# Down-projection LoRA and mix tables split once into DRAM during the gate/up pairs, and gathered ready-made two tiles ahead

## The reference

```
def lora_add(base, inp, A, B):
    t = einsum('bri,bni->bnr', A[idx], inp)
    return base + einsum('bor,bnr->bno', B[idx], t) * 0.5
gate = lora_add(x @ W_gate.T, x, A_gate, B_gate)        # 512 -> 1376
up   = lora_add(x @ W_up.T,   x, A_up,   B_up)
act  = silu(gate) * up
x = x + lora_add(act @ W_down.T, act, A_down, B_down)   # 1376 -> 512
x = x + einsum('bct,bcd->bdt', x, W[cond])              # 32 x 32 per sequence
```

## Time and profile before

| | us |
|---|---|
| median of 3 runs | 446.88 (446.78 to 447.9) |
| the profiled execution | 446.79 |
| its span in the trace | 445.0 |
| PE busy | 438.1 (98% of the span) |
| DVE busy | 335.2 (75%) |
| ACT busy | 212.3 (48%) |
| POOL busy | 169.7 (38%) |

### The profile page before, as it was taken

The page is one execution under the profiler, slowest core; times in us unless marked ns, Lnnn a source line. Parts: engine busy times, 40 slices in busy tenths (PEclk is TensorE's granted clock), DMA queues, the critical chain, the costliest instruction groups (busy, mean ns, idle before and its releaser), DMA issues.

```text
span 445.0 us, 7248 instructions
## 1 busy us (share of the span) xinstructions
PE 438.1 (98%) x2475; PEld 393.5 (88%) x2475; DVE 335.2 (75%) x623; ACT 212.3 (48%) x397; POOL 169.7 (38%) x156
## 2 busy tenths in 40 slices
PE   8989999999999999999999999999999999999997
PEld 6877888888888888888888888999999999999996
DVE  6779999878867867857857858978667767766665
ACT  6746355366444544543543444843454454444531
POOL 2722223121121221121121452675776666756620
PEclk9999999999999999999999999999999999999999
DMA  8975664356555665665565599947776665556631
GB/s 243 381 242 146 181 172 114 109 172 188 145 181 151 159 172 145 161 173 144 159 173 144 145 287 340 247 138 202 215 201 208 208 180 178 177 178 196 191 96 47
DMA packets 99843, 81.12 MB, mean 182 GB/s; under 512 B 50944, under 2 KB 83200, under 8 KB 99808
## 3 DMA queue, kind: packets, MB, share of 16 engines
q1 hardware_dynamic: 88512, 47.27, 37.9%
q0 software_dynamic: 11008, 33.30, 24.8%
q10 hardware_dynamic: 288, 0.10, 0.1%
HBM read 65.18 MB, written 15.47 MB: 181 GB/s over the span
## 4 chain that ended last, share of the span: by engine, by line
PE 92%; DMA 2%; POOL 2%; issue 2%; DVE 1%; ACT 1%; SPq 0%; POOLq 0%
PE bank L1384 28%; PE bank L1262 9%; PE bank L1263 9%; PE bank L1261 9%; PE bank L1216 7%; PE bank L1217 7%; PE bank L1218 7%; PE bank L1283 4%; PE bank L1284 4%; PE bank L1414 2%; POOL a_raw L453 2%; PE bank L1394 2%; DMA b_raw<-in_b_rows,rows 2%; DMA gu_landing<-in_w_gate 1%; PE bank L1399 1%
## 5 line engine op out<-in xcount | busy, mean ns | idle before, releaser
L453 POOL DMA_INDIRECT b_raw<-in_b_rows,rows x48 | 51.8, 1078 | 188.7 <-DVE b_gu L803 188.1
L1384 PE MATMUL bank<-wd,actT_hi 128*128 128x288 f32 (+1 forms) x636 | 109.9, 295 | 0.0
L1384 PEld LDWEIGHTS bank<-wd,actT_hi 128*128 128x128 f32 (+1 forms) x636 | 93.8, 188 | 1.4 <-issue 0.2
L453 POOL DMA_INDIRECT a_dn_raw<-in_a_dn_rows,rows x64 | 77.3, 1208 | 19.5 <-issue 19.5
L803 DVE SCALAR_TENSOR_TENSOR b_gu<-b_raw,low_rows,b_gu 128x1024 fp32r<-128x1024 f32 (+1 forms) x48 | 55.6, 1159 | 26.8 <-ACT b_gu L513 26.8
L1384 PE MATMUL bank<-wd,actT_lo 128*128 128x288 f32 (+1 forms) x318 | 68.1, 296 | 0.0
L513 ACT ACTIVATE b_gu<-b_raw 128x1024 fp32r<-128x1024 f32 (+1 forms) x48 | 46.2, 963 | 11.2 <-DMA b_raw<-in_b_rows,rows 9.8
L1384 PEld LDWEIGHTS bank<-wd,actT_lo 128*128 128x128 f32 (+1 forms) x318 | 51.0, 188 | 0.0
L603 ACT ACTIVATE act<-bank 128x512 f32<-128x512 f32 (+1 forms) x48 | 26.1, 546 | 41.4 <-PE bank L1284 41.4
L910 DVE TENSOR_TENSOR act<-act,bank 128x512 f32<-128x512 f32 (+1 forms) x48 | 29.8, 621 | 8.6 <-PE bank L1284 7.8
L799 DVE TENSOR_TENSOR actT_lo<-actT_raw,actT_hi 128x1280 fp32r<-128x1280 f32 (+1 forms) x32 | 27.0, 886 | 11.6 <-ACT actT_hi L513 11.6
(11 more groups left out here) (180 smaller groups left out, 1004.2 us busy)
## 6 DMA issues: line engine op xcount, KB each, us to landing
actT_raw<-actT_dram SPq DMA_DIRECT2D x16, 640.0 KB
actT_dram<-staging SPq DMA_DIRECT2D x64, 128.0 KB, 2.9
x_sb<-in_x SPq DMA_DIRECT2D x16, 256.0 KB, 2.9
xT_raw<-in_xT SPq DMA_DIRECT2D x15, 256.0 KB, 2.7
out<-out_sb SPq DMA_DIRECT2D x15, 256.0 KB
a_raw<-in_a_gu_rows SPq DMA_DIRECT2D x56, 64.0 KB, 2.7
actT_dram<-staging SPq DMA_DIRECT2D x32, 88.0 KB, 3.2
wd_raw<-in_w_down SPq DMA_DIRECT2D x10, 256.0 KB, 5.9
```

Of the source, the lines that this page charges most:

```text
L453: return pool.indirect_dma_start(dst, None, src, bass.IndirectOffsetOnAxis(ap=rows[:, tile, col:col + 1], axis=0))
L1384: last = pe.matmul(ps_down[e][half][:, 0:HALF], a[e][0:n, c, :], wd[0:n, c, part, at:at + HALF], start=(c == 0 and i == 0), stop=(c == NC ...
```

## The change

- **Tables.** Three internal DRAM tensors hold the high and the low part of all A_down rows (`a_table`, parts side by side in a row), all B_down rows (`b_table`, high rows and then low rows) and all mix matrices (`mix_table`). To the mix matrices the identity is added first, so the mix product gives `x + x W` in one.
- **Rounds.** The tables are made in seven rounds (`ROUNDS`): four of A_down (four adapters each, 128x704, 352 KB), two of B_down (128x512, 256 KB), one of the mix (128x128). A round is: SP loads it into `a_dn_raw[0]` (`load_round`), ACT writes the high part into `a_dn_raw[1]`, DVE writes the low part over `a_dn_raw[0]` (both `split_round`), SP stores both (`store_round`). All rounds use the same two buffers, so the load of a round waits until the stores of the one before it have landed (`tables_stored`).
- **Where they stand.** `rounds_of(pr)` gives pair 3 a late round 0, pair 4 an early round 1 and a late round 2, pair 5 rounds 3 and 4, pair 6 rounds 5 and 6. Early: on ACT after `split_b(pr, 1, 0)`, on DVE ahead of `gating(pr, 1)`. Late: on ACT ahead of `split_b(pr, 2, 0)`, on DVE after `add_u7`, ahead of `split_b(pr, 2, 0)`. SP stores the early round and loads the late one after `spill(pr, 0)`, and stores the late one and loads the next after `spill(pr, 1)`.
- **POOL.** The first gather of A_down, ahead of pair 7, waits until every round has been stored.
- **Down stage.** From tile 2 on the A_down rows come split from `a_table` into `a_pair` (two tiles ahead), and ACT only copies both parts; B_down comes split into `b_dn[e]`; the mix parts come by four DMAs of SP (`load_mix`, each with a register load). `split_b_dn`, `split_mix`, DVE's part of `split_a_dn` and `residual_out` are gone; ACT copies the output (`copy_out`). PE issues the same matmuls in the same order.

```diff
+            def load_round(i):
+                reached(sp, tables_stored, 32 * i)
+                if i < A_ROUNDS:
+                    sp.dma_start(a_dn_raw[0][:, :, :], a_round(i)).then_inc(table_landed, 16)
...
+            def store_round(i):
+                cols, tables = table_parts(i)
+                n = A_DN if i < A_ROUNDS else H if i < A_ROUNDS + 2 else CH
+                sp.wait_ge(table_ready, i + 1)
+                for part, to in enumerate(tables):
+                    src = table_sb(1 - part, cols, n if len(to.shape) == 3 else None)
+                    sp.dma_start(to, src).then_inc(tables_stored, 16)
...
+            def load_mix(m, e):
+                reached(sp, mix_done, 2 * (m - 1))
+                for q in range(TILE_SEQS):
...
                     spill(pr, s)
+                    if s == 0:
+                        if early is not None:
+                            store_round(early)
+                        if late is not None:
+                            load_round(late)
+                    else:
+                        if late is not None:
+                            store_round(late)
+                            if late + 1 < ROUNDS:
+                                load_round(late + 1)
...
             def gather_a_dn(m, q0=0, q1=TILE_SEQS):
-                reached(pool, a_dn_ready, m - 1)
+                if m == 0 and q0 == 0:
+                    pool.wait_ge(tables_stored, 32 * ROUNDS)
+                if m == 2:
+                    for t in range(2):
+                        pool.wait_ge(section_done[t], NS * PAIRS)
+                reached(pool, a_dn_copied, m - 3)
...
+            def split_round(i):
+
+                if i < ROUNDS - 1:
+                    sc.wait_ge(table_landed, 16 * (i + 1))
+                else:
+                    sc.wait_ge(table_mix_added, 1)
+                cols, _ = table_parts(i)
+                hi(table_sb(1, cols).bitcast(F32R), table_sb(0, cols)).then_inc(table_hi_ready, 1)
...
                     split_down(0, 3)
+                late = rounds_of(pr)[1]
+                if late is not None:
+                    split_round(late)
                 split_b(pr, 2, 0)
...
-            def split_mix(m, e):
...
+            def copy_out(m, e):
+                sc.wait_ge(mix_done, 2 * (m + 1))
+                reached(sc, stored[e], 16 * (m // 2))
+                hi(out_sb[e][:, :], ps_mix[:, 0:H]).then_inc(out_ready, 1)
```

More of the change, by code:

```diff
@@ L79, in build @@
         a_raw = [sb(f"a_raw{t}", [P, TILE_SEQS, A_GU]) for t in range(2)]
+        with ExitStack() as then:
+            a_pair = [sb(f"a_pair{e}", [P, TILE_SEQS, 2 * A_DN], F32, then) for e in range(2)]
         b_raw = [sb(f"b_raw{t}", [P, 2 * 512]) for t in range(2)]
@@ L497, in _ @@
                 pair(pr)
-            gather_mix(0)
+            gather(mix_raw[:, :], mix_rows, TILES - 1, 2 * TILE_SEQS + 2).then_inc(last_mix_landed, 16)
             pool.wait_ge(s_used, FAST)
-            gather_b_dn(0)
+            for m in range(2):
+                gather_b_dn(m)
+                gather_a_dn(m + 2)
             for m in range(2, TILES):
[L502 to L507, removed]
+                gather_b_dn(m)
+                if m + 2 < TILES:
+                    gather_a_dn(m + 2)
         @block.scalar
@@ L717, in split_a_dn @@
                 reached(sc, down_done, m - 1)
-                hi(wd_a(0, e), a_dn_raw[e][:, :, :].rearrange("p q (c r) -> p q c r", c=NC)).then_inc(a_dn_hi_ready, 1)
+                if m < 2:
+                    hi(wd_a(0, e), a_dn_raw[e][:, :, :].rearrange("p q (c r) -> p q c r", c=NC))\
+                        .then_inc(a_dn_hi_ready, 1)
+                else:
+                    for part in range(2):
+                        of = a_pair[e][:, :, part * A_DN:(part + 1) * A_DN]
+                        last = hi(wd_a(part, e), of.rearrange("p q (c r) -> p q c r", c=NC))
+                    last.then_inc(a_dn_copied, 1)
             def split_actT(m, e):
@@ L1077, in _ @@
             fast_pair(2, first=True)
+            for e in range(2):
+                nc.vector.memset(mix_w[e][:, :, :].bitcast(F32), 0.0).then_inc(mix_zeroed, 1)
             for pr in range(3, PAIRS - 1):
@@ L1560 @@
         "which": which,
-        "low": (p % (2 * RANK) >= RANK).astype(np.float32)[:, None],
+        "low": part.astype(np.float32)[:, None],
+        "eye": np.tile(np.eye(CH, dtype=np.float32), (TILE_SEQS, 1)),
     }
```

207 lines of the change are left out of this document (118 added, 89 removed).

## The result

| | median us | range | ratio to before, 95% |
|---|---|---|---|
| before | 446.85 | 446.78 to 447.9 | |
| changed | 473.56 | 472.07 to 476.86 | 1.060 [1.054, 1.066] |

The change costs 26.7 us; 460.5 was forecast, with 467 as the upper end. The direction was right, the size half. The medians of e3 and e9 further down hold one run each that was over 1.5% slower than the fastest of its kernel (477.37 and 464.16 us); without it they are 471.41 and 456.97 us.

What follows compares the result with a forecast made beforehand. PE, busy 438.1 of 445.0 us, was taken as the bound. Losses of 0.2, 4.2, 4.1 and 3.5 us in pairs 3 to 6 plus 1.7 at pair 7 made 13.7, on 446.8: 460.5 us, range 451 to 467.

Steps and rivals of the forecast that it cites:

- Removed work gives 0: Down stage: taking splits and a residual addition from DVE and ACT under a full PE saves 0 us.
- the down stage stays at 9.9 us a tile with a DMA share of 0.77: Down stage: SP's mix loads fit, doubled A rows are fetched two tiles ahead; added cost 0, DMA share perhaps 0.77.
- Early rounds give 0: Middle of a pair: ACT's 0.78 us and DVE's about 0.9 us of splitting are covered by PE; cost 0.
- SP begins the next pair's second part 1.0 us later against PE: Between late-round pairs: DVE catches up later in the pair, but SP starts the next pair's second part 1.0 us late.
- Late rounds lose L - 241.7: p3 of a pair: the split behind the late load delays PE; losses 0.2, 4.2, 4.1, 3.5 us in pairs 3 to 6.
- L: Landing time of the late round's load, on pair 6's clock; 245.9, 246.0, 245.2 in pairs 4 to 6.
- The clock, a rival at 0.10: PE's clock falls after each of four stalls, costing 2.1 us more each, 8.4 together: 469 us; chance 0.10.
- Matmuls longer than 0.23 us behind a stop: Sign in the profile, after a PE stall, that would show the forecast wrong.
- POOL and pair 7, 1.7 us: p1 of pair 7: POOL's B gather, behind the wait for all stores, comes late; 1.6 to 1.7 us on top.
- The longest wait of PE before: Kernel before: PE's longest listed wait is 1.7 us in all and lies in the first ten microseconds.
- DVE's lag behind them: After the p3 stop: DVE has no idle time until the next pair, lags by L - 240.7, less 1.0 of slack.

Runs made afterwards that it cites:

- e3: Changed kernel with 22, 20 and 8 idle-filling matmuls on PE ahead of the wait for b_gu in p3 of pairs 4, 5 and 6; 472.25 us.
- e9: Changed kernel with only the late round's split moved, on ACT behind split_b(pair, 2, 1), on DVE behind sum_x; 457.8 us.
- e4: Changed kernel with a third round buffer, separate store semaphores, low part stored first, late load ahead of spill(pair, 0), POOL's first gather waiting only for its buffer; 455.52 us.
- e8: e4 at the addresses of the kernel before, as in e7, with early stores and late load issued ahead of spill(pair, 0); 456.24 us.
- e7: Changed kernel with every tensor from low_rows on put back at its address in the kernel before; order and work untouched; 475.01 us.
- e6: Kernel before with an unused SBUF tensor of 1024 bytes a partition in front of low_rows; 447.87 us.
- e12: e9 with the tensors at the addresses of the kernel before, as in e7; 455.54 us.
- e2: Changed kernel without the rounds' loads, splits and waits; the 14 table stores stay, storing zeros and waiting for nothing; 455.61 us.
- e1: Kernel before with an unused SBUF tensor of 896 bytes a partition in front of low_rows; 450.62 us.
- e11: e10 with POOL's gather of tile 2's A rows moved ahead of the wait for s_used and gather_b_dn(0); 456.5 us.
- e10: e8 with the late round's split moved as in e9; 451.33 us.

## Why the prediction was wrong in size

- *Removed work gives 0; the down stage stays at 9.9 us a tile with a DMA share of 0.77.* Right: 9.93 and 0.76. One thing was missed, 1.0 us ahead of tile 2. The trace of before has a slow gather for this tile as well (5.92 us at 284.05), but there it is the second of four. With the change the first of them starts 1.3 us later against PE (308.26, less a lag of 24.3, where before had 282.65), is itself held for 5.9 us, and the set ends 1.1 us later. The prediction asked only how far ahead rows are fetched in the steady stage.
- *Early rounds give 0.* Right for their splits. But here stands **the step that failed first**: "SP begins the next pair's second part 1.0 us later against PE". The early round's load, too, waits on SP for two stores (waits of 5.5, 5.0 and 4.2 us ahead of pairs 4, 5 and 6), and everything of SP behind it, A rows, spill, stores and late load, was 3.3 us late in pair 4 (174.27 against 168.72 plus the creep of 2.2). In e4, where SP does not wait for these stores, it reaches the same place at 171.92. I had priced this wait for POOL's queue and for ACT's, and not for SP's own in the pair's second half.
- *Late rounds lose L - 241.7.* The formula's parts held: PE resumed at 187.53, 3.1 us after L = 184.4 (forecast L + 3.2). L itself was forecast at 245.9 on pair 6's clock, 181.9 in pair 4 with the creep; it came 2.5 later, which I put down to the reason above; no run changed that alone. So the stops were 5.2, 4.7 and 1.9 where 3.1, 3.2 and 2.4 would have followed from the forecast L. e9 shows that the place of the split, not the work in it, made them: with the same load time they are gone.
- *The clock, a rival at 0.10.* It came true, and not instead of the forecast but on top of it: 1.7, 2.0 and 1.6 us behind the three stops (forecast 2.1 each), 5.3 in all. I had argued that PE had never stood still so long in the trace of before; that says nothing about what it does when it does. Matmuls longer than 0.23 us behind a stop were also one of the prediction's own signs of being wrong. The price was taken from eight matmuls at the start, for which the profile's clock column reads 1.00; that such matmuls belong to the lower level is first shown by those behind the stops, 0.43 us apart at a granted 0.50. The Trainium skill says that a PE left idle by a DMA wait starts again at the lower clock (TensorE: Matmul & The Clock Gate, HAM oscillation). Behind the three p3 stops, which hang on a DMA through ACT and DVE, the rows agree: 0.58 behind 5.2 us of idle time, 0.50 behind 4.7, 0.59 behind 1.9. As a step of the sum, at its forecast price for three stops, it would have given 467.
- *POOL and pair 7, 1.7 us.* 1.6 at p1, as forecast, by the mechanism forecast. A second wait at p5 (DVE's `add_u3`, 1.5) was not seen.
- *The longest wait of PE before* lies at 27 us, not in the first ten as the prediction has it; its size, 1.5 us, stands, and no term hangs on it.
- *Nothing was said of the addresses*, 3.1 us. No step and no rival had it; the diff shows three lines of SBUF tensors changed and I read them as names only.

In sum 13.7 forecast; the three p3 stops with pair 7's first are 13.0 us of idle time, which is near it by luck, since the stops in pairs 4 and 5 were underpriced and DVE's lag behind them, priced at 1.1 a pair, was hidden under the low clock. Added to them: 6.2 more at the three p3 stops (5.3 of it low clock), 3.1 of addresses, and 2.9 more at pair 7 and tile 2, which makes the 25.3 but for rounding.

The Trainium skill gives some 2.0 us plus bytes over 436 GB/s for one DMA (DMA: Bandwidth & Descriptors, Anatomy of one DMA), fitted to transfers that GpSimd issues; these are issued by SP. By that estimate a 352 KB store would land in 2.8 us. Here the median is 5.1, and in e8 the load took 6.7: the measurement decides. That the difference comes from what stands ahead in the queue is my reading and wasn't tested by itself.

## What to carry to other kernels

Work for an engine with spare time costs what its place in a fixed order costs: behind a load that lands late, 0.8 us of splitting in each of three pairs held up everything behind it and cost 15.8 us; some places later it cost next to nothing. When two buffers and a wait for a store are put on a shared queue, price that wait for every item behind it in every round, not only in the one that you look at. And when a change adds SBUF tensors, compare the addresses of the matmul operands before and after, and put them back (e7) or pad (e6: 1024 bytes, the one distance that kept the speed here).

## What the runs showed of the hardware

- The speed of the 512-column float32 matmuls of the gate/up stage depends on where tensors lie in SBUF: 227 ns from start to start, 231 to 234 with the weights 896 or 3712 bytes higher, 227 with 1024. Those of 288 columns (132 ns) and 352 (160 in the mean) did not change. Matmuls on `b_gu`, which did not move, slowed as well, so it isn't simply the address of the matmul's own operand; the cause stays open.
- The length of a stop does not by itself say whether the clock falls. Behind 1.92 us (265.27) it did, and in e9 behind 1.23 us at 27.18; behind 1.36 us in e8 (182.48), 1.85 in e12 (27.37) and 2.56 in e2 (310.93) it did not. A window of e9 and one of e2, each from the end of its stop on:

```profile
27.20:33.00 5.80, 5.80 (x26) 5.16 (x27) 4.11 (x8) 1.95 (x4) 1.21 (x2) 0.71 0.47 137
```

```profile
310.93:315.00 4.07, 4.07 (x31) 4.07 (x32) 1.52 (x6) 0.83 (x3) 3.09 (x4) 1.00 1.00 263
```

- Behind the stop near 28 us, which nearly all kernels here have, the clock fell in six of the fourteen profiled executions (e1, e2, e7, e8, e9, e11) and cost about 1 to 3 us. It is no part of the change, and a difference of that size between two profiles has to be looked for there first.
- An indirect gather that takes POOL 0.95 us took 5.9 us (284.1 in the kernel before, 308.3 in the changed one) or 6.7 (e10) beside a run of DVE subtractions from SBUF to SBUF. In e10:

```profile
283.79 6.72 POOL L548 DMA_INDIRECT a_pair<-a_table,rows  x1 [0.89 <-PE bank L1388]
```

```profile
283.59 3.69 DVE L909 TENSOR_TENSOR wd<-wd_raw,wd 128x512 fp32r<-128x512 f32 x6
287.20 0.88 DVE L909 TENSOR_TENSOR wd<-a_dn_raw,wd 128x704 fp32r<-128x704 f32 x1
288.01 1.69 DVE L909 TENSOR_TENSOR actT_lo<-actT_raw,actT_hi 128x1280 fp32r<-128x1280 f32 x2
```

It ends at 290.5, just after that run. That the run holds it is read from the coincidence in these traces, and wasn't tested by itself.
